# Routed rows of a mixture-of-experts layer in 25 blocks of 256 and 21 blocks of 128 rows instead of 39 blocks of 256

## The chip, the cores and the metric

One core of one Trainium2 chip. The metric is the device time of one launch in microseconds (us).

## The reference, cut to what matters

A decoder layer on 16 x 256 = 4096 tokens of width 256: linear attention, cross attention to 77 context rows, and a feed-forward part with one shared expert and 8 routed ones, of which each token takes the best two. Only the last part is touched.

```python
for e in range(N_EXPERTS):                          # 8, hidden width 1024
    h = new_gelu(xf @ Wfc[e] + bfc[e]) @ Wproj[e] + bproj[e]
    routed = routed + h * gate[:, e:e + 1]          # gate is 0 but for the token's two experts
return shared + routed
```

## The kernel before

Three stages follow each other.

1. **Attention**, 16 steps, until about 266 us.
2. **Shared expert**, `NSH` = 16 blocks of 256 tokens. Beside it VectorE works out the routing in small parts (`route(part)`, one behind each of the first four slices of blocks 0 to 3): how many rows each expert gets, which block belongs to which expert (`blk_expert`) and at which row of a DRAM table `rows_by_expert` each token's two copies go. Then GpSimd sends the 64 half-tiles of rows there with indirect DMAs, spread by `gelu_done` over the shared blocks 4 to 14.
3. **Routed experts**, `NRT` = 39 blocks of 256 rows. The rows of an expert fill whole blocks, the last one of each expert with padding, so 2 x 4096 / 256 + 7 = 39 blocks hold every split of the rows. All 39 are always computed.

A block G runs through `FC` = 8 slices f of 128 hidden units. Its way **up** (TensorE, `up`) is six matmuls of 256 columns into one PSUM bank (two halves of the contraction, by three products of the high and low f16 parts). ScalarE applies gelu into `g32` (L697), VectorE splits the result into a high and a low f16 part (L973, L974; together a pair of buffers `gs[f % 4]`, `g_ready`). The way **down** (TensorE, `down`) is six matmuls of 256 columns, three for each tile of 128 rows, and runs two slices behind: up of slice f, then down of slice f - 2. Two PSUM banks (`hid[f % 2]`) hold what comes up, two (`ysum`) what goes down.

Around a routed block n (block G = 16 + n) stand these, each in the order of its engine's own instruction stream:

- VectorE, behind slice 2: `evacuate(G - 1)`: y = ysum / scale + b2 for both tiles (L945), `y_read`, then times the gate (L954), `y_ready`. Behind slice 6: it reads the next block's expert number and copies gates and token numbers out of `meta` (L994, L996), `meta_taken`.
- SyncE: load `meta` of a block (L458, waits for `meta_taken` of the block before it), then load its rows transposed (`load_xT`, L464, into `xT[n % 2]`, waits until block n - 2 is up), then `load_b2` of an earlier block (L432, waits for `y_read`). Since they stand in one stream, the rows of block n + 3 aren't asked for until VectorE has taken the meta of block n + 2 in block n + 1.
- GpSimd: wait for `y_ready` and for all adds before it, one small operation (L560), then for each tile an indirect DMA that adds 128 rows to the output (L563).
- TensorE reads the expert number at the start of a block (L1186), waits for `xT_loaded` and works out weight addresses on the way.

## Time and profile before

| | before |
|---|---|
| median of 3 runs | 862.61 us (862.16 to 863.20) |
| profiled execution | 864.7 us, of it span 863.0 us |
| busy TensorE / VectorE / ScalarE / GpSimd | 797.6 / 632.9 / 356.8 / 240.6 us |
| granted TensorE clock, mean | 0.97 |
| stages | attention to 266 us, shared blocks to 441.55, routed blocks to 852.1, tail to 863.0 |

The span is the profiler's window on the execution, the profiled time is 1.7 us longer. A busy engine is one with an instruction open; matmuls overlap in the records, so how fast they follow each other is read from the distance of their starts, not from their durations.

### The profile page before, as it was taken

The numbers are of one execution on the slowest core, as the hardware profiler recorded it, in microseconds if no ns is written. First come the engines' busy times: TensorE is split into PE (matmuls) and PEld (weight loads), VectorE is DVE, ScalarE is ACT, GpSimd is POOL, SyncE is SP. The second block draws the span as 40 slices with busy tenths as digits, with TensorE's granted clock in tenths as the row PEclk, the third lists the DMA queues.
The fourth block names the chain that finished last, engine by engine and source line by source line (L and its number), as shares of the span: only waits on it lengthen the run. The fifth ranks groups of instructions, "written<-read, shape, count | busy, mean of one in ns | idle before, by whom it ended". The sixth has DMA issues, their size and how long they took to land.

```text
span 863.0 us, 21653 instructions
## 1 busy us (share of the span) xinstructions
PE 797.6 (92%) x6791; PEld 671.2 (78%) x6791; DVE 632.9 (73%) x2006; ACT 356.8 (41%) x777; POOL 240.6 (28%) x221
## 2 busy tenths in 40 slices
PE   3889898899856999999999999999999999999994
PEld 1666676666644888888888888888888888888884
DVE  4578888988756998888876666666666666666663
ACT  4445454454323555555543333333333333333331
POOL 2210101101110025555503333333333333333333
PEclk9999999999956999999999999999999999999998
DMA  5465676765333567887743434355344434444430
GB/s 178 141 159 137 180 150 170 168 155 119 81 62 84 156 180 239 235 237 238 234 120 62 65 55 69 58 57 70 54 64 63 66 64 63 63 62 64 65 50 7
DMA packets 168045, 98.07 MB, mean 114 GB/s; under 512 B 110316, under 2 KB 163336, under 8 KB 167944
## 3 DMA queue, kind: packets, MB, share of 16 engines
q1 hardware_dynamic: 153640, 79.65, 38.3%
q0 software_dynamic: 14304, 17.10, 11.5%
q8 instruction: 61, 1.00, 0.5%
q14 instruction: 40, 0.33, 0.1%
HBM read 37.84 MB, written 37.88 MB: 88 GB/s over the span
## 4 chain that ended last, share of the span: by engine, by line
PE 67%; issue 22%; DVE 5%; DMA 2%; SPq 1%; ACT 1%; POOL 1%; POOLq 0%; DVEq 0%; ACTq 0%
PE bank_kv L1177 11%; PE bank_st L1163 11%; PE bank_kv L1179 11%; PE bank_st L1165 11%; PE bank_kv L1178 11%; PE bank_st L1164 11%; DMA stage_w<-in_L_ffn_Wfc_s 1%; POOL rstd L519 1%; DVE w_parts L961 1%; DVE w_parts L740 1%; PE bank_st L1097 1%; DVE expert_buffers L973 1%; DMA expert_buffers<-rows_by_expert 0%; SPq L345 0%; PE bank L1116 0%
## 5 line engine op out<-in xcount | busy, mean ns | idle before, releaser
L697 ACT ACTIVATE expert_buffers<-bank_st,bias_columns 128x256 f32<-128x256 f32 x440 | 207.0, 473 | 334.2 <-DVE expert_buffers L974 214.5
L1177 PE MATMUL bank_kv<-w_parts,expert_buffers 128*128 (+1 forms) x880 | 240.6, 273 | 1.0 <-DVE expert_buffers L974 1.0
L1178 PE MATMUL bank_kv<-w_parts,expert_buffers 128*128 (+1 forms) x880 | 240.4, 273 | 0.0
L1179 PE MATMUL bank_kv<-w_parts,expert_buffers 128*128 (+1 forms) x880 | 240.4, 273 | 0.0
L973 DVE TENSOR_SCALAR expert_buffers<-expert_buffers 128x256 f16<-128x256 f32 x440 | 130.2, 296 | 120.4 <-ACT expert_buffers L697 100.2
L974 DVE SCALAR_TENSOR_TENSOR expert_buffers<-expert_buffers 128x256 f16<-128x256 f32 x440 | 188.6, 429 | 15.1
L1163 PE MATMUL bank_st<-expert_buffers,w_parts 128*128 128x256 f16 x624 | 170.1, 273 | 1.3 <-DMA expert_buffers<-rows_by_expert 1.3
L1165 PE MATMUL bank_st<-expert_buffers,w_parts 128*128 128x256 f16 x624 | 170.1, 273 | 0.0
L1164 PE MATMUL bank_st<-expert_buffers,w_parts 128*128 128x256 f16 x624 | 170.1, 273 | 0.0
L563 POOL DMA_INDIRECT out<-expert_buffers,token x78 | 121.8, 1561 | 20.6 <-issue 20.2
L1177 PEld LDWEIGHTS bank_kv<-w_parts,expert_buffers 128*128 128x128 f16 x880 | 86.2, 98 | 15.1 <-DVE expert_buffers L974 2.9
L1179 PEld LDWEIGHTS bank_kv<-w_parts,expert_buffers 128*128 128x128 f16 x880 | 86.3, 98 | 10.3
L1178 PEld LDWEIGHTS bank_kv<-w_parts,expert_buffers 128*128 128x128 f16 x880 | 86.3, 98 | 9.9
L544 POOL DMA_INDIRECT rows_by_expert<-rows,dest_rows x64 | 66.6, 1041 | 96.2 <-ACT expert_buffers L697 82.9
L560 POOL TENSOR_TENSOR wait_carrier<-minus_half 128x1 f32<-128x1 f32 x39 | 17.5, 448 | 267.5 <-DVE expert_buffers L954 267.5
L519 POOL TENSOR_TENSOR rstd<-var_eps,minus_half 128x6 f32<-128x6 f32 x21 | 27.8, 1326 | 216.0 <-DVE var_eps L835 216.0
L1163 PE MATMUL bank_st<-w_parts 128*128 128x256 f16 x256 | 71.1, 278 | 0.0
L1164 PE MATMUL bank_st<-w_parts 128*128 128x256 f16 x256 | 71.0, 277 | 0.0
L1165 PE MATMUL bank_st<-w_parts 128*128 128x256 f16 x256 | 71.0, 277 | 0.0
L1163 PEld LDWEIGHTS bank_st<-expert_buffers,w_parts 128*128 x624 | 61.0, 98 | 8.6 <-issue 1.6
L1165 PEld LDWEIGHTS bank_st<-expert_buffers,w_parts 128*128 x624 | 61.1, 98 | 7.1
L1164 PEld LDWEIGHTS bank_st<-expert_buffers,w_parts 128*128 x624 | 61.1, 98 | 7.0
(150 smaller groups left out, 1027.0 us busy)
## 6 DMA issues: line engine op xcount, KB each, us to landing
rows_by_expert<-w_parts SPq DMA_DIRECT2D x13, 795.0 KB, 5.5
stage_w<-in_L_ffn_Wfc SPq DMA_DIRECT2D x16, 512.0 KB
stage_w<-in_L_ffn_Wproj SPq DMA_DIRECT2D x16, 512.0 KB
expert_buffers<-in_L_ffn_bproj SPq DMA_DIRECT2D x39, 128.0 KB
rows<-in_x SPq DMA_DIRECT2D x16, 256.0 KB, 3.2
x_residual<-rows SPq DMA_DIRECT2D x16, 256.0 KB, 4.7
expert_buffers<-x_residual SPq DMA_DIRECT2D x16, 256.0 KB
out<-expert_buffers SPq DMA_DIRECT2D x16, 256.0 KB
```

What stands on the lines that cost most here:

```text
L519: pool.tensor_tensor(rstd[:, :], var_eps[:, :], minus_half[:, :], ALU.pow)\
L544: pool.indirect_dma_start(out=rows_dram, out_offset=bass.IndirectOffsetOnAxis(ap=dest[:, j, t:t + 1].bitcast(U32), axis=0), in_=rows[:, t, ...
L563: pool.indirect_dma_start(out=out_rows, out_offset=bass.IndirectOffsetOnAxis(ap=token[slot][:, t:t + 1].bitcast(U32), axis=0), in_=ybuf[sl ...
L697: act.activation(g32[f % 2], hid[f % 2][:, 0:BLK], ACT.Gelu_apprx_tanh, bias=bias, scale=UNSCALE).then_inc(s["gelu_done"], 1)
L973: chain(dve.tensor_scalar(g[:, 0, :], g32[f % 2], A_SCALE, None, ALU.mult), "g_hi", c + 1)
L974: dve.scalar_tensor_tensor(g[:, 1, :], g32[f % 2], A_SCALE, g[:, 0, :], ALU.mult, ALU.subtract)\
L1163: pe.matmul(out_f, w_hi, x_hi, start=k == 0, stop=False)
L1164: pe.matmul(out_f, w_hi, x_lo, start=False, stop=False)
L1165: op = pe.matmul(out_f, w_lo, x_hi, start=False, stop=k == DK - 1)
L1177: pe.matmul(y, g[:, 0, tile(t)], w_hi, start=f == 0 and t == 0, stop=False, skip_group_check=True)
L1178: pe.matmul(y, g[:, 0, tile(t)], w_lo, start=False, stop=False, skip_group_check=True)
L1179: op = pe.matmul(y, g[:, 1, tile(t)], w_hi, start=False, stop=f == FC - 1, skip_group_check=True)
```

## The change

The 39 routed blocks of 256 become `FULL` = 25 blocks of 256 rows and `HALF` = 21 blocks of 128, 71 row tiles instead of 78. Each expert gets its full blocks first, and what remains of its rows in half blocks. 16 + 25 + 21 blocks run in one stream.

- In a half block the six matmuls up have 128 columns. The way down multiplies the high part by both weight parts side by side, in one matmul of 512 columns, and the low part by the high weights in one of 256: two matmuls a slice. It runs six slices behind (`LAG_HALF`).
- VectorE splits the gelu outputs of two slices at once (still 256 columns), and evacuates behind slice 5 in three dependent operations, since the two products now lie in separate halves of the bank. It takes the next meta behind slice 7.
- Ways up use four PSUM banks instead of two in all blocks.
- The routing has 20 parts instead of 16, reaching into shared block 4.
- The sends to `rows_by_expert` go over shared blocks 5 to 14 (10 blocks instead of 11); the last is released by the same gelu.
- The loops of SyncE and GpSimd over routed blocks are unrolled. 12 padding stores instead of 13.

```diff
-    NRT = 2 * T // BLK + E - 1
+    FULL = (2 * T - E * (BLK - 1) + BLK - 1) // BLK
+    HALF = 2 * T // P + E - 1 - FULL * TB
+    NRT = FULL + HALF
-    SEND_FROM, SEND_BLOCKS = 4, 11
+    SEND_FROM, SEND_BLOCKS = 5, 10
+        FIRST_HALF = NSH + FULL
+        LAG_FULL, LAG_HALF = 2, 6
@@ ScalarE @@
+                    if G >= FIRST_HALF:
+                        pair = (c - FC * FIRST_HALF) // 2
+                        spare = g32[pair % 2]
+                        at = slice(f % 2 * P, f % 2 * P + P)
+                        if f % 2 == 0:
+                            act.wait_ge(s["g_ready"], FC * FIRST_HALF + pair - 1 if pair < 2 else c - 2)
@@ VectorE, evacuate @@
+                if G >= FIRST_HALF:
+                    y = ybuf[parity][:, 0, :]
+                    chain(dve.scalar_tensor_tensor(y, ysum[parity][:, 0, :], UNSCALE, b2blk, ALU.mult, ALU.add),
+                          "y_part", G - FIRST_HALF + 1)
+                    dve.scalar_tensor_tensor(y, ysum[parity][:, 1, :], UNSCALE, y, ALU.mult, ALU.add)\
+                        .then_inc(s["y_read"], 1)
+                    dve.wait_ge(s["y_read"], G + 1)
+                    dve.tensor_scalar(y, y, gate[parity][:, 0:1], None, ALU.mult).then_inc(s["y_ready"], 1)
+                    return
@@ VectorE, body @@
-                    if isinstance(G, int) and G < 4 and f < 4:
+                    if G < 5 and f < 4:
                         route(4 * G + f)
-                    if f == 2 and not (isinstance(G, int) and G == 0):
+                    if f == (2 if G < FIRST_HALF else 5) and G > 0:
-                    if f == 6 and next_kind(G, routed) == "routed":
+                    if f == (6 if G < FIRST_HALF else 7) and next_kind(G, routed) == "routed":
@@ TensorE @@
-                if not (isinstance(c, int) and c < 2):
-                    pe.wait_ge(s["gelu_done"], c - 1)
+                if c >= 4:
+                    pe.wait_ge(s["gelu_done"], c - 3)
+                if G >= FIRST_HALF:
+                    g = gs[(c - FC * FIRST_HALF) // 2 % 4][:, :, f % 2 * P:f % 2 * P + P]
+                    y = bank_kv[:, parity, :].rearrange("p (l n) -> p l n", l=2)
+                    both = w2[:, ds(e * 4096 + ((f // 4) * 2048), 2048)].rearrange("p (l n) -> p l n", l=2)
+                    both = both[:, :, (f % 4) * 256:(f % 4) * 256 + D]
+                    pe.matmul(y, g[:, 0, :], both, start=f == 0, stop=False, skip_group_check=True)
+                    pe.matmul(y[:, 0, :], g[:, 1, :], both[:, 0, :], start=False, stop=f == FC - 1, skip_group_check=True)\
+                        .then_inc(s["down_done"], 1)
+                    return
```

**Routing parts.** Before, `route` had 24 operations, now 41. Of the 17 added, 13 work on 8 columns (one count for each expert), three on 256 columns (whether a row lies beyond the full blocks, and the jump that it then makes), and the comparison that gives `blk_expert` is cut in two (200 and 168 columns where there was one of 312).

How the change stands in the instruction streams. TensorE, in a routed block before: the end of a way up, the way down of the slice two behind, the next way up (`bank_st` is `hid`, `bank_kv` is `ysum`).

```order
L1165 MATMUL bank_st<-expert_buffers,w_parts 128x256
L1177 REGISTER_ALU [waits g_ready]
L1177 MATMUL bank_kv<-w_parts,expert_buffers 128x256
L1178 REGISTER_ALU
L1178 MATMUL bank_kv<-w_parts,expert_buffers 128x256
L1179 MATMUL bank_kv<-w_parts,expert_buffers 128x256
L1177 MATMUL bank_kv<-w_parts,expert_buffers 128x256
L1178 MATMUL bank_kv<-w_parts,expert_buffers 128x256
L1179 MATMUL bank_kv<-w_parts,expert_buffers 128x256
L1163 ISA [waits gelu_done]
L1163 MATMUL bank_st<-expert_buffers,w_parts 128x256
```

The same place in a half block:

```order
L1249 MATMUL bank_st<-expert_buffers,w_parts 128x128
L1263 REGISTER_ALU [waits g_ready]
L1263 MATMUL bank_kv<-w_parts,expert_buffers 128x512
L1264 MATMUL bank_kv<-w_parts,expert_buffers 128x256
L1247 ISA [waits gelu_done]
L1247 MATMUL bank_st<-expert_buffers,w_parts 128x128
L1248 MATMUL bank_st<-expert_buffers,w_parts 128x128
L1249 ISA
L1249 MATMUL bank_st<-expert_buffers,w_parts 128x128
L1247 ISA
L1247 MATMUL bank_st<-expert_buffers,w_parts 128x128
```

Six matmuls down of 256 columns have become one of 512 and one of 256; those up still carry a weight load and every second one an address operation (ISA), and have half the columns.

VectorE in a routed block before, from the split of slice 3 to that of slice 6 and the taking of meta (L989 to L994); the evacuation stands right ahead of the first of these rows:

```order
L973 TENSOR_SCALAR expert_buffers<-expert_buffers 128x256 [waits down_done,gelu_done]
L974 SCALAR_TENSOR_TENSOR expert_buffers<-expert_buffers 128x256 [waits g_hi]
L973 TENSOR_SCALAR expert_buffers<-expert_buffers 128x256 [waits down_done,gelu_done]
L974 SCALAR_TENSOR_TENSOR expert_buffers<-expert_buffers 128x256 [waits g_hi]
L973 TENSOR_SCALAR expert_buffers<-expert_buffers 128x256 [waits down_done,gelu_done]
L974 SCALAR_TENSOR_TENSOR expert_buffers<-expert_buffers 128x256 [waits g_hi]
L973 TENSOR_SCALAR expert_buffers<-expert_buffers 128x256 [waits down_done,gelu_done]
L974 SCALAR_TENSOR_TENSOR expert_buffers<-expert_buffers 128x256 [waits g_hi]
L989 TENSOR_LOAD block_expert
L989 ISA x2
L994 ISA [waits y_added,meta_loaded]
L994 COPY gate<-expert_buffers 128x2
```

VectorE in a half block, from the split of slices 4 and 5:

```order
L1055 TENSOR_SCALAR expert_buffers<-expert_buffers 128x256 [waits down_done,gelu_done]
L1057 SCALAR_TENSOR_TENSOR expert_buffers<-expert_buffers 128x256 [waits g_hi]
L1010 SCALAR_TENSOR_TENSOR expert_buffers<-bank_kv,expert_buffers 128x256 [waits y_added,b2_loaded,down_done]
L1012 SCALAR_TENSOR_TENSOR expert_buffers<-bank_kv,expert_buffers 128x256 [waits y_part]
L1015 TENSOR_SCALAR expert_buffers<-expert_buffers,gate 128x256 [waits y_read]
L1055 TENSOR_SCALAR expert_buffers<-expert_buffers 128x256 [waits down_done,gelu_done]
L1057 SCALAR_TENSOR_TENSOR expert_buffers<-expert_buffers 128x256 [waits g_hi]
L1072 TENSOR_LOAD block_expert
L1072 ISA x2
L1078 ISA [waits y_added,meta_loaded]
L1078 COPY gate<-expert_buffers 128x1
L1080 COPY token<-expert_buffers 128x1
```

There were four splits between the last operation of the evacuation and the taking of meta; now there is one, and the three operations of the evacuation (L1010, L1012, L1015) each wait for the one before.

SyncE before, one turn of its loop: meta of a block, its rows transposed, and the expert number for the b2 of the block before:

```order
L457 REGISTER_ALU
L458 ISA [waits meta_taken]
L458 DMA expert_buffers<-rows_by_expert 128x2x9
L463 ISA
L464 ISA [waits up_done]
L464 DMA_TRANSPOSE expert_buffers<-rows_by_expert 128x4x256
L468 ISA
L468 TENSOR_LOAD block_expert
```

SyncE in the half blocks:

```order
L492 DMA expert_buffers<-rows_by_expert 128x9 [waits meta_taken]
L500 DMA_TRANSPOSE expert_buffers<-rows_by_expert 128x4x128 [waits up_done]
L504 TENSOR_LOAD block_expert
L504 ISA x2
L466 ISA [waits y_read]
L466 DMA expert_buffers<-in_L_ffn_bproj 128x256
```

The order of the three loads is the same, the address operations are gone, and the transposed tile has 128 rows instead of 256.

## Rows read from the trace of the kernel before

**Rows 1.** The page: busy time of each engine, share of the span, instructions.

```profile
PE 797.6 (92%) x6791; PEld 671.2 (78%) x6791; DVE 632.9 (73%) x2006; ACT 356.8 (41%) x777; POOL 240.6 (28%) x221
```

**Rows 2.** Busy by stretch (PE, PEld, DVE, ACT, POOL, clock, DMA, GB/s): routed, shared.

```profile
620.00:710.00 90.00, 90.00 (x827) 80.65 (x826) 60.68 (x190) 32.50 (x69) 28.62 (x25) 1.00 0.41 64
...
292.00:302.50 10.50, 10.13 (x93) 8.76 (x92) 10.09 (x27) 5.27 (x10) 0.00 (x0) 1.00 0.49 153
302.50:313.00 10.50, 10.04 (x93) 8.76 (x91) 10.06 (x28) 5.58 (x10) 0.00 (x0) 1.00 0.52 164
```

**Rows 3.** Timeline of TensorE (start, length in us): the same matmul of two successive blocks.

```profile
600.39 0.27 PE L1163 MATMUL bank_st<-expert_buffers,w_parts 128*128 128x256 f16 x1
...
610.87 0.27 PE L1163 MATMUL bank_st<-expert_buffers,w_parts 128*128 128x256 f16 x1
```

**Rows 4.** Timeline of TensorE in one attention step: matmuls of other widths.

```profile
155.45 0.45 PE L1140 MATMUL bank<-w_parts 128*128 128x8 f16 x12
...
159.53 0.39 PE L1059 MATMUL bank<-w_parts 128*128 128x77 f16 x6
159.76 2.75 PE L1069 MATMUL bank_kv<-w_parts 128*128 128x512 f16 x12
162.35 1.47 PE L1076 MATMUL bank<-w_parts 128*128 128x256 f16 x12
```

**Rows 5.** Source lines L1140 and L1059: durations ns min/median/max of one instruction.

```profile
L1140 PEld LDWEIGHTS bank<-w_parts x192: 95/96/147, 73.8 to 265.8; 128*128 128x128 f16 x192
L1140 PE MATMUL bank<-w_parts x192: 166/166/211, 74.0 to 265.8; 128*128 128x8 f16 x192
...
L1059 PE MATMUL bank<-w_parts x192: 196/199/267, 50.6 to 250.6; 128*128 128x77 f16 x192
```

**Rows 6.** Timeline of VectorE in a routed block.

```profile
603.50 0.75 DVE L945 SCALAR_TENSOR_TENSOR expert_buffers<-bank_kv,expert_buffers 128x256 f32<-128x256 f32 x2
604.29 0.62 DVE L954 TENSOR_SCALAR expert_buffers<-expert_buffers,gate 128x256 f32<-128x256 f32 x2
604.82 0.29 DVE L973 TENSOR_SCALAR expert_buffers<-expert_buffers 128x256 f16<-128x256 f32 x1
...
605.48 0.29 DVE L973 TENSOR_SCALAR expert_buffers<-expert_buffers 128x256 f16<-128x256 f32 x1
...
608.40 0.43 DVE L974 SCALAR_TENSOR_TENSOR expert_buffers<-expert_buffers 128x256 f16<-128x256 f32 x1
609.23 0.17 DVE L994 COPY gate<-expert_buffers 128x2 f32 x1 [0.40 <-DMA out<-expert_buffers,token]
609.30 0.16 DVE L996 COPY token<-expert_buffers 128x2 int32<-128x2 int32 x1
```

**Rows 7.** ScalarE's groups: busy us, mean ns of one | idle before.

```profile
L697 ACT ACTIVATE expert_buffers<-bank_st,bias_columns 128x256 f32<-128x256 f32 x440 | 207.0, 473 | 334.2 <-DVE expert_buffers L974 214.5 <-PE bank_st L1165 108.3 <-issue 11.3
L580 ACT ACTIVATE w_parts<-bank 128x154 f32<-128x154 f32 x16 | 4.7, 294 | 3.3 <-PE bank L1107 3.3
```

**Rows 8.** SyncE's queue, timeline of DMA issues.

```profile
440.47 0.37 SPq L458 DMA_DIRECT2D expert_buffers<-rows_by_expert  x1
440.89 1.24 SPq L464 DMA_TRANSPOSE expert_buffers<-rows_by_expert  x1
...
609.64 0.38 SPq L458 DMA_DIRECT2D expert_buffers<-rows_by_expert  x1
```

**Rows 9.** DMA issues of the span: median us from issue to landing.

```profile
expert_buffers<-rows_by_expert SPq DMA_TRANSPOSE x39, 3.2
...
w_parts<-rows SPq DMA_TRANSPOSE x32, 2.5
```

**Rows 10.** Timeline of GpSimd: the last block's adds.

```profile
854.00 1.56 POOL L563 DMA_INDIRECT out<-expert_buffers,token  x1
855.86 1.55 POOL L563 DMA_INDIRECT out<-expert_buffers,token  x1 [0.30 <-issue]
```

**Rows 11.** VectorE's groups: two routing operations, on 256 and on 8 columns.

```profile
L906 DVE TENSOR_TENSOR w_parts<-w_parts 128x256 f32<-128x256 f32 x1 | 0.4, 421 | 0.0
...
L900 DVE TENSOR_SCALAR w_parts<-w_parts 128x8 int32<-128x8 int32 x1 | 0.2, 172 | 0.0
```

More of the change, by code:

```diff
@@ L60, in decoder_layer, with tiles_in, rows_of, sent @@
     PADS = 3
[L61 to L63 removed]
+    SEND_FROM, SEND_BLOCKS = 5, 10
+    PAD_STEPS = (ROW_TILES + PADS * TB - 1) // (PADS * TB)
+    assert FULL == 25 and HALF == 21 and PAD_STEPS < B
     assert S == 256 and D == 256 and H == 1024 and CK <= P
[L66 to L67 removed]
+    rows_dram = nc.dram_tensor("rows_by_expert", [PAD_STEPS * PADS * TB * P, ROW], F32).ap()
+    rows16_dram = rows_dram.bitcast(F16)[:, 0:2 * D]
     x2_dram = nc.dram_tensor("x2_residual", [T, D], F32).ap()
+    def tiles_in(n):
+        return TB if n < FULL else 1
+    def rows_of(n):
+        first = n * BLK if n < FULL else FULL * BLK + (n - FULL) * P
+        return slice(first, first + tiles_in(n) * P)
+    def sent(n):
+        return sum(tiles_in(m) for m in range(n)) * 16
     def tiles_of(ap, b):
@@ L223, in decoder_layer @@
         base = scratch(TE).rearrange("p (e t) -> p e t", e=E)
+        beyond = gated
         place = te(scratch(TE))
@@ L1191, in body @@
                 e = expert_of(G - NSH) if routed else E
-                if before != "routed":
-                    e_before = E
-                else:
-                    e_before = expert_of(G - (NSH + 1)) if at_start else held[0]
-                held[0] = e
+                experts[G] = e
+                lag = LAG_FULL if G < FIRST_HALF else LAG_HALF
                 for f in range(FC):
@@ L1202, in body @@
                     up(G, parity, e, f)
-                    if f >= 2:
-                        down(G, parity, e, f - 2)
-                    elif before is not None:
-                        down(G - 1, 1 - parity, e_before, FC - 2 + f)
+                    d = FC * G + f - lag
+                    if d >= 0 and not (G == FIRST_HALF and f < LAG_HALF - LAG_FULL):
+                        down_lagging(d)
                     if f == 1 and isinstance(G, int) and G == 0:
@@ L1216, in body @@
                 if is_last(G):
-                    for f in range(FC - 2, FC):
-                        down(G, parity, e, f)
+                    for d in range(FC * NBLK - lag, FC * NBLK):
+                        down_lagging(d)
             pe.wait_ge(s["x1_ready"], B)
```

195 lines of the change are left out of this document (121 added, 74 removed).

## The prediction

> **What bounds the kernel now.** I read the busy times first, then the stretches, then the timelines of single engines. TensorE is busy for 797.6 of 863.0 us, VectorE for 632.9 [rows 1]. The stretches say where that matters: from 620 to 710 us TensorE is busy for 90.00 of 90.00 us at a granted clock of 1.00, VectorE for 60.68 and GpSimd for 28.62; in the shared blocks around 300 us VectorE is busy for 10.09 of 10.50 us and TensorE already stands still for 0.37 [rows 2]. So the routed stage is bound by TensorE alone, and the part of the shared stage that carries the routing is bound by VectorE. The timeline of TensorE gives the price of a routed block: the same matmul comes 10.48 us later in the next block [rows 3], which is 96 matmuls of 256 columns at 109.2 ns from start to start. All 39 blocks are the same.
>
> **What is removed.** 39 blocks become 25 of the same kind. 14 x 10.48 = 146.7 us go.
>
> **What a half block costs TensorE.** It has 48 matmuls up of 128 columns, 8 down of 512 and 8 of 256. No row shows one of 128 columns in f16, so I bound its distance from the rows at other widths. For 512 columns it is (162.35 - 159.76) / 12 = 215.8 ns [rows 4]; with 109.2 for 256 that is 106.6 ns for each 256 columns and 2.6 ns besides. So 128 columns take 53.3 + 2.6 = 55.9 ns, if nothing else shows up when matmuls get short. What could is the weight load, since each matmul has its own. The rows with short matmuls speak to that: twelve of 8 columns fill 0.45 us, the last being 0.166 long, so they start 0.284 / 11 = 26 ns apart, each with its load of a full 128 x 128, which is recorded as 96 ns long; six of 77 columns start (0.39 - 0.199) / 5 = 38 ns apart, 6 ns over their 32 ns of columns [rows 4, 5]. Loads of 96 ns thus overlap. With those 6 ns I get 59.3 as the other end for 128 columns. I take 55.9, since the matmuls here stand in long runs like the ones of 256. A half block is then 48 x 0.0559 + 8 x (0.2158 + 0.1092) = 2.68 + 2.60 = **5.28 us** (5.45 at the other end). The five address operations of a slice have half the time of before to run ahead in. They were hidden before, and I add nothing for them; the first rival prices them together with the weight loads.
>
> **What a half block needs around it.** The block has half the time, but the chain that brings in the next rows doesn't halve. Rows of block n + 3 are asked for by SyncE only behind the meta of block n + 3, and that waits until VectorE has taken the meta of block n + 2 behind slice 7 of block n + 1. I follow it from the start of slice 5 in block n + 1:
> - gelu of slice 5 done after about 1.0 us: matmuls up 0.34, the way through the array and a semaphore about 0.3, gelu 0.37 (473 ns at 256 columns, a copy of 154 columns takes 294 [rows 7]; an estimate between them)
> - VectorE: the split of slices 4 and 5, 0.66 until the next operation may start (604.82 to 605.48); the evacuation, whose operations overlapped in pairs (0.75 for two, 0.62 for two) and now each wait for the one before, about 1.2; the split of slices 6 and 7, 0.75; reading the expert number and the two copies, 0.40 + 0.23 [rows 6]
> - SyncE: 0.18 until the meta is issued (609.46 to 609.64), 0.42 until the transposing load (440.47 to 440.89) [rows 8]
> - the load: 3.2 us from issue to landing for 256 rows, 2.5 for the transposes of 128 rows in the attention stage [rows 9]; I take 2.5, since the size is the same, though those start in SBUF and these in DRAM
> - 0.1 until TensorE starts.
>
> That is 7.5 us, from a point 5 x 0.66 = 3.3 us into block n + 1, and the end is the start of block n + 3. Two blocks can't be shorter than 10.8 us, one not than **5.4**. That is 0.12 more than TensorE needs. So I expect TensorE to wait a little for its rows at each half block: 21 x 5.4 = 113.4 us. If the landing is under 2.2 the chain is covered and it is 21 x 5.28 = 110.9; with the landing of 3.2 and 0.2 more on SyncE it is 5.85 and 122.9. Behind the waiting TensorE nothing else is late, since every other chain hangs on it. VectorE itself has about 4 x 0.66 + 1.2 + 0.64 = 4.5 us of work for each half block, GpSimd one add, which starts 1.86 us after the one before where two follow each other [rows 10], and about 0.7 ahead of it: both below 5.4.
>
> **Routing.** VectorE gets 13 more operations on 8 columns at 0.172 + 0.04 of waiting, three on 256 columns at 0.42 + 0.04 [rows 11], and about 0.3 for the comparison cut in two: 2.75 + 1.4 + 0.3 = 4.4 us. They fall into shared blocks 1 to 4, where VectorE has 0.4 us to spare in 10.5 [rows 2]. Nothing hides them there but the slack of about 1 us that the way down has, two slices behind, and block 4, which had no routing before. Of the four blocks I count 8 x 0.66 = 5.3 us of splits, 1.5 of evacuation and 2.5 of weight conversion each, 37.2 together (10.09 of 10.50 with some routing among it [rows 2]); with the routing of before, 6.3 by its groups, and the added 4.4 it is 47.9 against 41.9 us of TensorE's work, 6.0 over, where three blocks were 2.8 over before. TensorE's added wait is **+3.2 us**, with 2 and 4.4 as bounds. Below nothing it can't go.
>
> **The end.** The last block has one add instead of two; the second started 1.86 us behind the first [rows 10], and both lie behind the last matmul. **-1.9 us.** The six slices of lag at the end are matmuls that are counted already. They wait for the split of slices 6 and 7 about as long as the old ones did: 0. The sends end behind the same gelu as before, and one padding store less lies beside the attention: 0. Four PSUM banks change nothing for full blocks, where TensorE didn't wait: 0.
>
> **Sum.** -146.7 + 113.4 + 3.2 - 1.9 = -32.0. The profiled execution (864.7, span 863.0) would become 832.7 and 831.0; on the median of 862.6, which lies 0.4 us below the span and 2.1 below its own time, it gives **830.6 us**.
>
> **Rivals.**
> - *The matmuls of 128 columns show part of their weight loads.* Halfway between 55.9 ns and the recorded length of a load, at 76 ns, a half block takes 48 x 0.076 + 2.60 = 6.25 us, 21 of them 131.2, and the kernel 862.6 - 146.7 + 131.2 + 3.2 - 1.9 = 848.4. For it: no row has this width, and TensorE's address operations stand between the loads. Against it: 26 and 38 ns at shorter widths. The Trainium skill, page "TensorE: Matmul & The Clock Gate", section "Back-to-back issue gap", gives about 81 ns for a sustained stream of load and matmul at 128 columns, against 56 for isolated ones; by it a half block would take 6.49 us and the kernel 853. By that rule much of the gain would go, though this trace's 38 ns at 77 columns speak against it.
> - *They show them in full, and the kernel gets slower.* At 96 ns, the recorded load, a half block takes 7.21 us, 21 take 151.4, more than the 14 full ones gave, and the kernel 868.6. It decides from (146.7 + 1.9 - 3.2) / 21 = 6.92 us for a half block, 90 ns a matmul. The same rows speak against it.
> - *The chain of loads is longer than I count it*, because the landing stays near 3.2 us or VectorE comes late: 5.85 us, 862.6 - 146.7 + 122.9 + 3.2 - 1.9 = 840.1. The load runs beside adds, meta and b2 loads that are as many for half the rows.
> - *Nothing waits*: 5.28 us and routing at its lower bound of 2: 826.9.
>
> **How the numbers follow.** The forecast's own case, 827.5 to 835, has 0.60; the longer chain, 835 to 842, 0.14; loads partly shown, 842 to 861, 0.12; slower 0.06; under 827.5, 0.08. The range of 826 to 848 leaves out the slower case, the upper half of the loads' case and the last bit below, some 0.16. Changes under 0.2% can't be told from none here. Faster by more: 0.93. Within: 0.01. Slower: 0.06.
>
> **What would show it.** Half blocks 5.3 to 5.5 us apart in TensorE's timeline, matmuls up 56 to 59 ns apart. Where TensorE idles, it is at the start of a half block, released by the DMA of `rows_by_expert`, about 0.1 us a time; waits in the middle of a block, for `g_ready` or gelu, would show the chain wrong. Full blocks still 10.48 us. Shared blocks 1 to 4 together 3 us longer, with VectorE busy throughout. One add behind the last matmul. The prediction fails if the distance of matmuls up is over 65 ns, or the landing of the half transposes over 3 us.

## The result, and the profile after

The changed kernel takes 849.89 us (median of 4 runs, 847.65 to 851.07) against 862.38 us before: ratio 0.985, 95% interval 0.9817 to 0.9883. That is faster, by 12.5 us where the prediction had 32, and outside its range of 826 to 848. The profiled execution took 847.65 us, of it span 845.9.

The page after, busy times (beside [rows 1]):

```profile
PE 769.6 (91%) x6791; PEld 628.9 (74%) x6791; DVE 627.3 (74%) x1988; ACT 365.7 (43%) x833; POOL 228.6 (27%) x221
```

The stretches after (columns as in [rows 2]): full routed blocks, two shared blocks, half blocks.

```profile
620.00:710.00 90.00, 90.00 (x844) 80.59 (x843) 61.78 (x190) 33.32 (x73) 29.09 (x25) 1.00 0.42 64
292.00:302.50 10.50, 9.77 (x89) 8.17 (x87) 9.98 (x29) 5.10 (x9) 0.00 (x0) 1.00 0.52 143
302.50:313.00 10.50, 9.16 (x81) 7.29 (x80) 9.95 (x28) 5.09 (x9) 0.00 (x0) 1.00 0.45 133
710.00:835.00 125.00, 114.96 (x1290) 86.30 (x1288) 84.17 (x265) 59.12 (x161) 39.37 (x42) 1.00 0.40 61
```

Full blocks are what they were. In the half blocks TensorE stands still for 10 of 125 us, at the full clock (granted 1.00, which is 2.4 GHz), and no other engine is full. Where it stands still, its timeline shows (the start of a half block, and the second slice behind it):

```profile
760.02 0.38 PE L1263 MATMUL bank_kv<-w_parts,expert_buffers 128*128 x1
760.24 0.27 PE L1264 MATMUL bank_kv<-w_parts,expert_buffers 128*128 x1
760.94 0.23 PE L1247 MATMUL bank_st<-expert_buffers,w_parts 128*128 128x128 f16 x1 [0.43 <-DMA expert_buffers<-rows_by_expert]
761.00 0.22 PE L1248 MATMUL bank_st<-expert_buffers,w_parts 128*128 128x128 f16 x1
761.06 0.23 PE L1249 MATMUL bank_st<-expert_buffers,w_parts 128*128 128x128 f16 x1
761.19 0.23 PE L1247 MATMUL bank_st<-expert_buffers,w_parts 128*128 128x128 f16 x1
...
761.75 0.22 PE L1247 MATMUL bank_st<-expert_buffers,w_parts 128*128 128x128 f16 x1
761.80 0.22 PE L1248 MATMUL bank_st<-expert_buffers,w_parts 128*128 128x128 f16 x1
761.86 0.22 PE L1249 MATMUL bank_st<-expert_buffers,w_parts 128*128 128x128 f16 x1
761.91 0.22 PE L1247 MATMUL bank_st<-expert_buffers,w_parts 128*128 128x128 f16 x1
761.97 0.22 PE L1248 MATMUL bank_st<-expert_buffers,w_parts 128*128 128x128 f16 x1
762.02 0.22 PE L1249 MATMUL bank_st<-expert_buffers,w_parts 128*128 128x128 f16 x1
762.08 0.38 PE L1263 MATMUL bank_kv<-w_parts,expert_buffers 128*128 x1
```

In a long run the matmuls of 128 columns start 0.055 us apart, the one of 512 holds the array for 0.22 and that of 256 for 0.11: the array time of the prediction. A slice is 0.66, eight are 5.28. But between two blocks there is a gap, 0.70 us from the last matmul down to the first up where 0.11 would do, and the first slice behind it is slower by 0.15 (0.81 from 760.94 to 761.75). From start to start half blocks take 6.10 us in the median, 6.19 in the mean (18 intervals; the first two, 5.34 and 6.32, in which the stage of full blocks ends, are left out here and below). The row names the rows' DMA as releaser of 0.43 us. The waits of TensorE and of its weight loads between 710 and 835 us put most down to something else (total us, times, longest):

```profile
PEld bank_st L1247 <- issue: 17.8, 21, 1.9
```
```profile
PE bank_st L1247 <- DMA expert_buffers<-rows_by_expert: 6.2, 9, 1.5
PE bank_st L1247 <- ACT expert_buffers L733: 3.6, 10, 0.4
```

"Issue" stands at the start of each of the 20 half blocks behind the first (at one of them twice), so the profile shows nothing that the weight load waited for: TensorE's own instruction stream was late. What stands there is the read of the expert number, L1284. Its line in the trace, in half blocks and around 760 us after, then in full blocks and around 608 us before (PEldq is the stream, durations in ns):

```profile
L1284 PEldq TENSOR_LOAD <-block_expert x19: 296/302/642, 715.5 to 827.4; - x19
L1284 PEldq FUSED_REGOPS  x19: 151/151/151, 716.2 to 827.7; - x19
L1284 PEldq SEQ_ASSERT  x19: 18/18/18, 716.5 to 827.9; - x19
...
L1284 PEldq TENSOR_LOAD <-block_expert x1: 302/302/302, 760.0 to 760.0; - x1
L1284 PEldq SEQ_ASSERT  x1: 18/18/18, 760.6 to 760.6; - x1
```
```profile
L1186 PEldq TENSOR_LOAD <-block_expert x1: 577/577/577, 607.8 to 607.8; - x1
L1186 PEldq SEQ_ASSERT  x1: 26/26/26, 608.6 to 608.6; - x1
```

Before, the read began at 607.8 and the block's first matmul at 609.23: the stream was 1.4 us ahead of the array, and the read, longer than after, was hidden. After, it begins at 760.0, as the last way down enters the array (760.02 and 760.24). It ends at 760.6, and the array restarts at 760.94. The stream has lost its lead. What fills it in the half blocks, besides matmuls and loads, are address operations (line L1249, 710 to 830 us):

```profile
L1249 PEldq FUSED_REGOPS  x310: 46/46/46, 710.4 to 829.9; - x155
```

L1247 has as many, so a slice has four of them, with one of 32 ns for the way down: 4 x 46 + 32 = 216 ns in a slice of 660. The starts of these operations show the lead in every slice. Before, an address operation of L1163 begins 0.5 us ahead of its matmul in slice 0, right behind the read, and 0.8 to 1.2 us ahead from slice 2 on (medians): the stream wins its lead back. In the half blocks it is 0.10 us in slice 0 and 0.2 to 0.4 in slices 1 to 7, and it hardly grows there.

**Where the time went**, by the two traces: from the start of the first half block (705.07) to the end of the last matmul (836.54) it is 131.5 us; the last full block before ran 1.9 us past its 10.48, so the half blocks cost 129.6 us, not 113.4. The shared stage is 2.3 us longer (175.74 to 178.00 from the first matmul up of shared block 0 to that of routed block 0; blocks 1 to 4 +3.6, block 0 -2.5, the others +1.1). The last matmul's end to the span's end fell from 10.9 to 9.4; the attention is 0.7 shorter. -146.7 + 129.6 + 2.3 - 1.5 - 0.7 = -17.0, and the spans differ by 17.1. The medians differ by 12.5 alone, because the profiled execution lies 2.3 us above its median before and 2.2 below it after.

### The profile page after: what moved, and what is told of

The parts are those of the page before. It is cut to its first block, busy times and chain, and to the rows that moved or that the text cites. A ratio compares the mean times of both kernels' runs of the same rounds, so it can differ in the third digit from the quotient of the medians.

```text
span 845.9 us, 21759 instructions
## 1 busy us (share of the span) xinstructions
PE 769.6 (91%) x6791; PEld 628.9 (74%) x6791; DVE 627.3 (74%) x1988; ACT 365.7 (43%) x833; POOL 228.6 (27%) x221
## 4 chain that ended last, share of the span: by engine, by line
PE 51%; issue 25%; DVE 10%; DMA 10%; ACT 2%; POOL 1%; SPq 1%; POOLq 0%; ACTq 0%; DVEq 0%
PE bank_kv L1270 7%; PE bank_kv L1271 7%; PE bank_kv L1272 7%; PE bank_st L1247 5%; DMA expert_buffers<-rows_by_expert 5%; PE bank_st L1249 4%; PE bank_st L1248 4%; PE bank L1247 4%; PE bank L1249 4%; PE bank L1248 4%; PE bank_kv L1263 3%; DMA stage_w<-in_L_ffn_Wproj 2%; DVE w_parts L1034 2%; DVE expert_buffers L1047 2%; PE bank_kv L1264 1%
## 5 line engine op out<-in xcount | busy, mean ns | idle before, releaser
L1270 PE MATMUL bank_kv<-w_parts,expert_buffers 128*128 (+1 forms) x656 | 179.0, 273 | 5.0 <-DVE expert_buffers L1048 4.7
L733 ACT ACTIVATE expert_buffers<-bank_st,bias_columns 128x256 f32<-128x256 f32 (+1 forms) x248 | 108.1, 437 | 166.3 <-PE bank_st L1249 119.2
L1272 PE MATMUL bank_kv<-w_parts,expert_buffers 128*128 (+1 forms) x656 | 178.8, 273 | 0.0
L1271 PE MATMUL bank_kv<-w_parts,expert_buffers 128*128 (+1 forms) x656 | 178.8, 273 | 0.0
L733 ACT ACTIVATE expert_buffers<-bank,bias_columns 128x256 f32<-128x256 f32 (+1 forms) x248 | 108.2, 436 | 142.2 <-PE bank L1249 76.6
L1047 DVE TENSOR_SCALAR expert_buffers<-expert_buffers 128x256 f16<-128x256 f32 x328 | 101.7, 310 | 78.1 <-ACT expert_buffers L733 76.9
L1048 DVE SCALAR_TENSOR_TENSOR expert_buffers<-expert_buffers 128x256 f16<-128x256 f32 x328 | 139.4, 425 | 11.3
L1247 PE MATMUL bank_st<-expert_buffers,w_parts 128*128 128x256 f16 (+1 forms) x368 | 88.3, 249 | 11.3 <-DMA expert_buffers<-rows_by_expert 7.5
L1249 PE MATMUL bank_st<-expert_buffers,w_parts 128*128 128x256 f16 (+1 forms) x368 | 88.4, 249 | 0.0
L1248 PE MATMUL bank_st<-expert_buffers,w_parts 128*128 128x256 f16 (+1 forms) x368 | 88.0, 248 | 0.0
L1249 PE MATMUL bank<-expert_buffers,w_parts 128*128 128x256 f16 (+1 forms) x368 | 87.1, 248 | 0.0
L1248 PE MATMUL bank<-expert_buffers,w_parts 128*128 128x256 f16 (+1 forms) x368 | 87.0, 248 | 0.0
L1247 PE MATMUL bank<-expert_buffers,w_parts 128*128 128x256 f16 (+1 forms) x368 | 87.0, 248 | 0.0
L1270 PEld LDWEIGHTS bank_kv<-w_parts,expert_buffers 128*128 128x128 f16 x656 | 64.1, 98 | 17.4 <-DVE expert_buffers L1048 9.6
L1272 PEld LDWEIGHTS bank_kv<-w_parts,expert_buffers 128*128 128x128 f16 x656 | 64.2, 98 | 7.5
L1271 PEld LDWEIGHTS bank_kv<-w_parts,expert_buffers 128*128 128x128 f16 x656 | 64.2, 98 | 7.1
L1263 PE MATMUL bank_kv<-w_parts,expert_buffers 128*128 x168 | 63.3, 378 | 0.5 <-DVE expert_buffers L1057 0.5
L1153 PE MATMUL bank_kv<-w_parts 128*128 128x512 f16 x192 | 47.6, 401 | 13.2 <-DMA w_parts<-w_parts 13.2
```

The costliest lines, as they stand in the source:

```text
L733: act.activation(spare[:, at], hid[c % 4][:, 0:width(G)], ACT.Gelu_apprx_tanh, bias=bias, scale=UNSCALE).then_inc(s["gelu_done"], 1)
L1047: chain(dve.tensor_scalar(g[:, 0, :], g32[f % 2], A_SCALE, None, ALU.mult), "g_hi", c + 1)
L1048: dve.scalar_tensor_tensor(g[:, 1, :], g32[f % 2], A_SCALE, g[:, 0, :], ALU.mult, ALU.subtract)\
L1247: pe.matmul(out_f, w_hi, x_hi, start=k == 0, stop=False)
L1248: pe.matmul(out_f, w_hi, x_lo, start=False, stop=False)
L1249: op = pe.matmul(out_f, w_lo, x_hi, start=False, stop=k == DK - 1)
```

## The experiments

Theories for the half block's 6.1 us. **A**: TensorE's own stream, that is the read of the expert number behind address operations that leave it no lead. **B**: the chain that brings the rows (meta, then transposed rows), longer than the prediction's 7.5 us; in this trace the transposing loads land after 2.9/3.4/4.8 us (min/median/max) where it took 2.5. The expectations have letters of their own. In runs 1, 2 and 5 theory A is the chain (B here) and B the loads themselves; S in runs 5 to 9 is A here; the stream was first put down as a theory for run 5, after runs 1 and 2 had come out against the chain.

Half blocks are given as mean and median from start to start. A static expert, or one read used for all half blocks, makes the half blocks multiply by another expert's weights. Only times of neighbouring runs compare well: the attention ends at 263 to 268 us in these traces, and in runs 5 to 9 the shared blocks 4 to 15 exceed their 10.48 us by 8.5 to 9.9 us in sum, in runs 1 to 4 and 10 by 2.9 to 5.4 (run 12 comes back to that). So the times of runs 5 to 9 are some 5 us longer for reasons outside the half blocks; what a run does to the half blocks is read from its trace.

**1. The rows asked for first.** SyncE's order in routed blocks:

```diff
                 load_xT(n + 2)
+                load_rows(n + 2)
                 load_b2(n + (1 + NSH), expert_of(n + 1))
-                if n + 3 < NRT:
-                    load_rows(n + 3)
```
(with the `load_rows(2)` ahead of the loop gone). The meta of block n + 2 then stands behind its rows.

> SyncE asks for the transposed rows of a block before the meta of that block, so that the load no longer waits for VectorE. Theory A (TensorE's waits in the half blocks come from the chain VectorE evacuates, splits, takes meta, then SyncE loads meta, then rows, which is 8.6 us long from slice 5 and closes over two blocks): the load is then issued when the block two ahead is up, has 5.3 us for 3.4 to 3.8 us, and half blocks come every 5.3 to 5.35 us instead of 6.2: 20 x 0.9 = 18 us less than the changed kernel, about 831. Theory B (the loads themselves, or the DMA engines, can't follow at this rate): half blocks stay above 5.9 us and the time above 844.

844.73 us, ratio 0.9793 (0.9753 to 0.9834), and not the 831 of the chain's theory. Half blocks 6.06/6.06: the outliers of up to 7.2 us are gone, the median hardly moved. The waits between 710 and 830 us:

```profile
PEld bank_st L1245 <- issue: 14.8, 20, 1.1
```

No wait for the rows' DMA is left, and the block's start is as late as ever. B explains the outliers, not the 6.06.

**2. Four slices behind instead of six**, the evacuation behind slice 3, which shortens the chain.

```diff
-        LAG_FULL, LAG_HALF = 2, 6
+        LAG_FULL, LAG_HALF = 2, 4
-                    if f == (2 if G < FIRST_HALF else 5) and G > 0:
+                    if f == (2 if G < FIRST_HALF else 3) and G > 0:
```

> The way down of the half blocks runs four slices behind instead of six, and VectorE evacuates behind slice 3 instead of 5, so that the evacuation no longer stands between the last gelu of a block and the taking of meta. Theory A: the split of slices 6 and 7 starts when its gelu is done, about 0.56 us earlier, the chain over two blocks is shorter by that, a half block by 0.28 (6.2 to 5.9): about 6 us less, 844, if the shorter lag brings no wait for the way down. Theory B (loads or DMA engines are the limit): no change, 850.

844.33 us, 0.9776 (0.9738 to 0.9814), half blocks 6.08/6.07. As in 1. The time is the one that the chain's theory named, but by luck: its half blocks were to take 5.9.

**3. Half blocks without their adds.** Leaves out the indirect DMAs that add the half blocks' rows to the output.

```diff
-                for t in range(tiles_in(n)):
+                for t in range(tiles_in(n) if n < FULL else 0):
```

> Leaves out the adds of the half blocks into the output (GpSimd's indirect DMAs of 21 blocks), so the output lacks those rows; all else stays. If the transposing loads land after 3.4 us instead of 2.5 because the add of the evacuated block runs beside them, they land after about 2.5, half blocks take 5.6 to 5.75 and the kernel about 839 with the missing last add. If the landing is the load's own, it stays at 3.3 to 3.4, half blocks at 6.0 to 6.1, and the time at 845 to 848.

842.48 us, 0.9776 (0.9736 to 0.9817). The transposes land faster, and half blocks stay at 6.11/6.06:

```profile
DMA to landing us min/median/max: 2.7/2.7/4.5
```

So the adds do lengthen the landing, from 2.7 us to the 3.4 of the changed kernel. That isn't what holds the array.

**4. One routing operation four times** (on 256 columns, in block 3), to see whether routing work is paid in full.

```diff
+                    for _ in range(4):
                         then(dve.tensor_tensor(beyond, place, over_t(full_rows), ALU.is_ge))
```

> One wide routing operation of VectorE in shared block 3 is done four times instead of once: 3 x 0.46 = 1.4 us more. If VectorE bounds the shared blocks with routing, blocks 1 to 4 take 1.4 us longer in TensorE's timeline and the kernel 851.3. If the added routing has slack to lie in, under 0.4 us.

850.01 us, 0.9876 (0.9818 to 0.9933). Block 3 took 13.81 us instead of 12.43: +1.38 for three operations of about 0.46. The whole shared stage took 178.59 us where runs 1 and 2, on the same chip, have 177.16 and 177.14: VectorE's added work there is paid one to one. The kernel's median moved by 0.1 us alone; 1.4 us lie within the scatter of its four runs (849.15 to 857.06).

**5. A static expert for TensorE in half blocks**, the order of SyncE as in the changed kernel. This removes the read and all the address operations.

```diff
-                e = expert_of(G - NSH) if routed else E
+                if G >= FIRST_HALF:
+                    e = G % E
+                else:
+                    e = expert_of(G - NSH) if routed else E
```

> On TensorE alone the half blocks use a fixed expert number (G modulo 8) instead of the one read from memory, so TensorE neither reads the number nor works out addresses in them; the output of those blocks is that of another expert. Theory A (the chain of VectorE and the loads of rows sets the half block, 8.6 us over 5.3 of lead): half blocks stay at 6.0 to 6.2 us, 850. Theory S (TensorE's own instruction stream sets it: reading the expert number takes 0.6 us at the start of each block, and the stream, with an address operation for every second or third matmul, doesn't get far enough ahead of the array to hide it): the 0.7 us at the block's start go, until the chain of the rows, 0.2 to 0.4 us behind it, is the limit: 5.6 to 5.85 us, about 842.

847.41 us, 0.9771 (0.9704 to 0.9839); half blocks 6.02/5.76. The waits of the weight loads from 710 to 835 us:

```profile
PEld bank_st L1247 <- DMA expert_buffers<-rows_by_expert: 15.4, 14, 2.7
...
PEld bank_st L1247 <- issue: 0.2, 1, 0.2
```

The wait on "issue" is gone and the rows' chain has taken its place, at 5.8 us in the median, with outliers up to 7.8: a second limit right behind the first. Behind such gaps, of up to 2.3 us, the first six matmuls up take 0.34 us, where they take 0.49 to 0.64 in the changed kernel. So the address operations themselves make the block's first slice longer, by 0.15 us or more.

**6. Both: static expert and rows first.**

> The same fixed expert number on TensorE in the half blocks, and SyncE asks for the rows before the meta. Theory S: both limits are gone, half blocks at 5.28 to 5.35 us, 21 x 0.75 under the rows-first kernel's 844.7: about 830. Theory D (the DMA landings, at 3.4 us, or VectorE, are the limit left): 5.6 or more, over 835.

831.89 us, 0.9605 (0.9565 to 0.9645); half blocks 5.33/5.28. With both limits out of the way most half blocks take exactly their array time. That the kernel also comes near the predicted 830.6 us is partly luck: its half blocks are 0.1 us under the predicted 5.4, and its shared blocks 4 to 15 exceed 10.48 us by 9.1 us where the changed kernel's trace has 4.5.

**7. The read ahead of slice 3 of the block before**, rows first: is it enough to read earlier?

```diff
+                    if f == 3 and FIRST_HALF <= G < NBLK - 1:
+                        experts[G + 1] = expert_of(G + 1 - NSH)
                     up(G, parity, e, f)
```
(and the block's start uses what was read.)

> Rows first, and TensorE reads the next half block's expert number ahead of slice 3 of the block before, addresses as before. If only the place of the read mattered (at the start of a block, where it meets the wait for the rows), the 0.6 us would be hidden and half blocks take 5.3 to 5.5: about 833. If the stream of instructions is the limit as a whole, the same 0.7 us come back in the middle of the block: 6.0 us, 844.

849.58 us, 0.9814 (0.9776 to 0.9852), half blocks 6.09/6.03. The slices' medians were 0.825, five or six of 0.66, 0.695, 1.195 in run 1; here 0.715, 0.66, 1.095, 0.81, 0.66, 0.66, 0.71, 0.66. The stall moved with the read, to the start of slice 3, and the waits of the weight loads from 710 to 830 us still say "issue":

```profile
PEld bank L1245 <- issue: 12.7, 20, 0.7
```

An earlier place doesn't help where the stream has so little lead anywhere: address operations begin 0.2 to 0.4 us ahead of their matmuls in most slices here too. Nor is it that the block's addresses wait for the number: the next block needs it only some 4 us later. The slices clear of the read still take 0.66 to 0.72 us, address operations and all.

**8. One read for all half blocks**, rows first. It was meant to take the read away and keep the address operations.

```diff
-                e = expert_of(G - NSH) if routed else E
+                if G > FIRST_HALF:
+                    e = experts[FIRST_HALF]
+                else:
+                    e = expert_of(G - NSH) if routed else E
```

> Rows first, and TensorE reads an expert number once, for the first half block, and uses it for all 21; the address operations stay. The output is that of another expert. Theory S: without the read the stream needs less than the array's 5.28 us: 5.3 to 5.45, about 831 to 834. If the address operations are the larger part, 5.6 to 5.9 and about 840.

840.60 us, 0.9716 (0.9667 to 0.9765); half blocks 5.64/5.29. But the trace shows that the address operations went with the read. A line of the ways up between 710 and 830 us (the changed kernel has 310 such operations on it, above):

```profile
L1247 PEldq FUSED_REGOPS  x8: 46/46/46, 710.1 to 712.6; - x8
```

All eight lie ahead of the second half block; with one number for all half blocks the addresses are worked out once. For TensorE this run is run 6 over again, and it doesn't separate the two. Twelve of 18 half blocks take 5.28 to 5.30; the others wait for the rows:

```profile
PEld bank_st L1245 <- DMA expert_buffers<-rows_by_expert: 7.9, 7, 1.5
```

Seven of its transposing loads landed after 4.4 to 5.1 us. Why these are so slow here and not in run 6 is not shown.

**9. The read kept, its result unused, no address operations**, rows first.

```diff
                 e = expert_of(G - NSH) if routed else E
+                if G >= FIRST_HALF:
+                    e = G % E
```

> Rows first; TensorE reads the expert number at the start of each half block but doesn't use it: addresses are those of a fixed expert, without address operations (the output of those blocks is another expert's). Theory S says that the read (about 0.65 us) and the address operations (8 x 4 x 46 + 8 x 32 ns = 1.7 us) are both in the way only together: without the operations the stream runs far enough ahead to hide the read, and half blocks take 5.28 to 5.4 us, 832. If the read stops the array by itself (because it waits until the queue is empty, say), 0.6 us stay: 5.9 us, 844.

839.68 us, 0.9712 (0.969 to 0.9735), half blocks 5.35/5.28. The line of the read in half blocks, and around 760 us:

```profile
L1282 PEldq TENSOR_LOAD <-block_expert x21: 296/306/594, 713.3 to 819.4; - x21
...
L1282 PEldq TENSOR_LOAD <-block_expert x2: 297/300/302, 760.0 to 765.6; - x2
```

It reads as long as in the changed kernel, but begins 1.6 us ahead of its block (761.64), and 1.2 us or more in all; with the address operations it is 0.85 to 0.9 in most blocks, and the gap itself is part of that: there the read begins only 0.2 us ahead of the last matmul down, here 1.1 to 1.5. **So the read costs nothing where no address operations stand beside it** (9). Read and address operations together cost 6.05 - 5.28 = 0.77 us a half block, 16 us in 21 (run 1 against 6 and 9). Theory A holds, and B is the limit right behind it. No run has the address operations without the read. That they alone would be hidden over a whole block is likely, since in run 1 the six slices between the one behind the gap and the one ahead of the next take 0.66 to 0.70 us, but it is not shown.

The time of 839.68 us is 7.8 over run 6's with the same half blocks. In the traces 3.8 us of it are a longer attention, 0.8 the shared blocks, and 1.7 the first routed block, which waits for its rows.

**10. Rows first and four slices behind.**

> The changed kernel with the rows of block n + 2 asked for ahead of its meta of n + 3 (as in the run with rows first) and the half blocks' way down four slices behind with the evacuation behind slice 3 (as in the run with four slices). Theory A (the read of the expert number in TensorE's stream is exposed and sets 6.05 us per half block once the rows' chain is out of the way): no further gain, 843 to 845 us, half blocks 6.05 us. Theory B (the chain of rows still gave part of the 6.05): 838 to 841 us, half blocks below 5.9 us.

845.56 us, 0.9811 (0.9759 to 0.9863), half blocks 6.06/6.06: nothing beyond 1 or 2, as A has it. Runs 1, 2 and 10 are the best kernels here that leave nothing out, 18 to 19 us under the kernel before.

**11. Routing thinner, sends denser**: three parts of the routing in each of blocks 1 to 6, the sends over 8 blocks (7 to 14), rows first.

```diff
-    SEND_FROM, SEND_BLOCKS = 5, 10
+    SEND_FROM, SEND_BLOCKS = 7, 8
-                    if G < 5 and f < 4:
+                    elif 1 <= G < 7 and f in (0, 1, 3) and 3 * G + (0, 1, 3).index(f) + 1 < 20:
```

> Rows first, and the routing behind block 0 goes with three parts a block over shared blocks 1 to 6 instead of four a block over 1 to 4, with the sends over blocks 7 to 14. VectorE then has 6 blocks for the same work: by the theory that it bounds those blocks, TensorE's added wait of 4.9 us in blocks 1 to 4 falls to about 3, so the kernel is 1.5 to 2.5 us under the rows-first one (844.7, so 842 to 843), unless the denser sends cost it elsewhere.

859.96 us, 0.9963 (0.9943 to 0.9983), 17 us over what was expected. Blocks 1 to 6 exceed 10.48 us by 3.1 us in sum where run 1 had 5.0, so thinner routing gains 1.9. Blocks 7 to 14, with the denser sends, exceed it by 16.8. That raised a question on the change itself, whose four banks and ten blocks of sends the prediction counted at nothing.

**12. Those two edits alone in the kernel before.**

```diff
-    SEND_FROM, SEND_BLOCKS = 4, 11
+    SEND_FROM, SEND_BLOCKS = 5, 10
-        hid = [bank_st[:, c, :] for c in range(2)]
+        hid = [bank_st[:, 0, :], bank_st[:, 1, :], bank3[:, :], bank7[:, :]]
-                    pe.wait_ge(s["gelu_done"], c - 1)
+                    pe.wait_ge(s["gelu_done"], c - 3)
```
(and `hid[f % 4]` where it was `hid[f % 2]`). In the expectations from here on S means that the sends are the cause, K the banks, J only both together, and C the chip.

> The kernel before with two parts of the change alone: four PSUM banks for the way up, and the sends over blocks 5 to 14 instead of 4 to 14. Prediction of record: nothing, 862.6 +- 1. If the denser sends cost what the changed kernel shows in shared blocks 6 to 12 (1.1 us more than before), 863.7.

869.09 us, 1.007 (1.0049 to 1.0092): slower by 6 us. Then each alone, on another chip:

> The kernel before with its sends to rows_by_expert over shared blocks 5 to 14 (10 blocks) instead of 4 to 14, and nothing else; two PSUM banks for the ways up as before. Together with four banks this cost about 6 us (869.1 against 863.2). Theory S (the denser sends alone lengthen the shared blocks): about 868 to 869 us, the shared blocks with sends exceed 10.48 us by some 7 us in sum. Theory K (the four banks are what does it): 863 us, excess about 1.3 us as in the kernel before. Theory J (only both together): 863 here and in the run with four banks alone.

> The kernel before with four PSUM banks for the ways up in all blocks, sends over blocks 4 to 14 as before, and nothing else. Theory S: 862.5 to 863, no change. Theory K: 868 to 869 us, the shared blocks with sends exceed 10.48 us by some 7 us in sum. Theory J: 863.

863.95 us, 0.9999 (0.9975 to 1.0024), for the sends, 864.85 us, 1.0023 (0.9998 to 1.0049), for the banks. But the changed kernel in run 10, on the same chip, lost no more in its shared blocks than these two, so the chip could have been the reason. Hence the kernel before itself, with a trace, beside both edits, on one chip:

> The kernel before itself, unchanged, so that its trace and that of the next run come from one chip. Its shared blocks 4 to 15 exceeded 10.48 us by 2.8 us in sum in the trace that the prediction read. Theory C (how much the shared blocks lose is a property of the chip: the traces of the two other chips with 8 to 10 us lost it in every kernel): this sum lies within 1.5 us of that of the next run. Theory J (four banks and sends over ten blocks together lose it): about 3 to 5 us here.

> The kernel before with four PSUM banks for the ways up and the sends over blocks 5 to 14, as in the run that was 6 us slower on another chip. Theory J: again 1.005 to 1.009 of the kernel before, the shared blocks 4 to 15 exceed 10.48 us by some 8 us. Theory C: within 0.3% of the kernel before, with its sum of excess.

865.11 us, 1.0014 (0.9987 to 1.0041), and 871.31 us, 1.0075 (1.0051 to 1.0098); excess of blocks 4 to 15 over 10.48 us: 4.6 and 10.6. The waits for VectorE's splits at the way down, from 300 to 445 us, of the one and of the other:

```profile
PEld bank_kv L1177 <- DVE expert_buffers L974: 2.5, 8, 0.7
```
```profile
PEld bank_kv L1177 <- DVE expert_buffers L974: 12.1, 23, 1.4
```

Both edits together cost 6 us on such a chip, as J has it, and C is right in part: chips differ. The gaps between GpSimd's sends tell them apart (its line, idle without a releaser, us and times: the kernel before itself and both edits, then the sends alone):

```profile
  issue: 12.2, 34
```
```profile
  issue: 14.9, 43
```
```profile
  issue: 5.8, 19
```

Across the traces the gaps are 4 to 8.5 us on some chips (changed kernel, runs 1 to 4, 10, each edit alone) and 11 to 16 on the others (kernel before, runs 5 to 9, 11 and 12's both edits). The runs went over six chips, with two to four traces on each, all of one kind. On which chip the traces of the kernel before and of the changed kernel in the sections above were taken isn't known. Kernels with both edits (without run 11) exceed 10.48 us in blocks 4 to 15 by 2.9 to 5.4 us on the first and by 8.2 to 10.6 on the second. Each edit alone once more, on a chip of the first kind again:

> The kernel before with the sends over blocks 5 to 14 and nothing else, again, since on the chip of its first run nothing lost time in the shared blocks. Chips fall into two kinds by the gaps between GpSimd's sends: in some traces 5 to 8 us of gaps with no releaser before the 64 sends, in others 11 to 16. If this chip is of the second kind: theory J (only both edits together) 1.000 of before and an excess of the shared blocks 4 to 15 over 10.48 us of 3 to 5.5 us; theory S (the sends) 1.005 to 1.009 and 8 to 10.6 us. If it is of the first kind, as in its first run: 1.000 and about 5 us by either.

> The kernel before with four PSUM banks and nothing else, again. On a chip of the second kind: theory J 1.000 of before and an excess of 3 to 5.5 us; theory K (the banks) 1.005 to 1.009 and 8 to 10.6 us. On one of the first kind: 1.000 to 1.002 and about 5 us by either.

864.49 us, 1.0007 (0.9978 to 1.0037), and 862.26 us, 0.9989 (0.996 to 1.0018), with 2.9 and 1.8 us of excess. Whether one edit alone costs something on a chip of the second kind stays open, as does what the chips differ in.

## Why the prediction was right in sign and wrong in size

- **"14 x 10.48 = 146.7 us go"**: right, full blocks are 10.48 us still.
- **The array time of a half block, 5.28 us**: right, 48 matmuls up at 55 ns and 0.66 a slice; run 6 shows it undisturbed. The rival of weight loads that show comes near the measured time (848.4) by luck, for a reason that isn't there: in long runs matmuls of 128 columns stand 55 ns apart. The Trainium skill, page "TensorE: Matmul & The Clock Gate", section "Back-to-back issue gap", has about 81 ns a matmul for a sustained stream of weight loads and matmuls at 128 columns; the trace doesn't agree, with 55 ns.
- **"The five address operations of a slice have half the time of before to run ahead in. They were hidden before, and I add nothing for them"**: this is the step that failed. The words name the danger and then price it at nothing. The read of the expert number at the block's start, which the description of the kernel names, has no term at all. Together they cost 0.77 us a half block, 16 us (run 1 against runs 6 and 9), because with 128 columns the stream's lead stays at 0.2 to 0.4 us where it was 0.8 to 1.2, and the read with what belongs to it takes 0.47 and more. With the address operations gone the read is hidden (run 9); whether they would be hidden without the read is open.
- **The chain of rows, 5.4 us a half block**: mis-sized. It is 5.8 in the median (run 5), because the landing is 3.3 us there and 3.4 in the changed kernel, and not 2.5 (0.7 of the 3.4 from the adds, run 3), which is the rival with 5.85. It cost only the outliers here, about 21 x 0.13 = 3 us, since TensorE's stream is later still. The other links came as predicted: evacuation 1.18 us (760.12 to 761.30) for 1.2, reading and copies 0.40 + 0.22, SyncE 0.37 between the two loads.
- **Routing, +3.2 us**: +3.6 in blocks 1 to 4, and added work there is paid one to one (run 4). The match is in part luck: block 0 has 2.5 us less wait than in the trace that the prediction read. In sum over blocks 0 to 4 the excess rose from 5.2 to 6.4 us; in six of the eight traces of the kernel before, with run 12's edits or none, it is 3.5. So routing added between 1.2 and 2.9 us.
- **The end, -1.9**: -1.5.
- **"Four PSUM banks change nothing for full blocks, where TensorE didn't wait: 0"**, and the sends: 0. For the changed kernel's own trace this nearly holds, its shared blocks 5 to 15 exceed 10.48 us by 3.9 us where they had 2.8. On some chips both together cost 6 us in the shared blocks (run 12), where TensorE is not the only full engine. The prediction had looked at the routed blocks for the banks and at the last send for the sends.
- **What would show it**: "waits 0.1 us at the start of a half block, released by the DMA" was the wrong releaser and size; the text also said that it fails with a landing over 3 us, which came.

## What to carry to other kernels

In these traces TensorE's instruction stream runs ahead of the array by a lead (up to 1.4 us before, 0.2 to 0.4 in the half blocks), and register work is hidden only as far as that lead goes. When a change halves the matmuls' length but not their number, or the register work beside them, work out the stream's time too: from the line of each register read (PEldq here) take how far ahead of its block it begins, and ask what is left of it when the array needs half the time. Look at the trace of each experiment for whether its edit did what it was meant to: run 8's took away more. And where two limits lie within 0.3 us of each other a run that removes one shows only the other; take both away in one kernel, then put each back.

## What the runs showed of the hardware that was not expected

- A register read on TensorE's stream took 0.30 us and the operations behind it 0.15 and 0.02; from its start to the array's restart it was 0.85 to 0.9 us in most blocks (changed kernel). 32 address operations of 46 ns and 8 of 32 ns a half block of 128-column matmuls kept its lead at 0.2 to 0.4 us; beside matmuls of 256 columns it recovered to 0.8 to 1.2 us within two slices.
- Behind the gap the first six matmuls of 128 columns take 0.48 us (760.94 to 761.42), later six 0.33. It isn't the array that restarts slowly: with no address operations they take 0.34 behind gaps of up to 2.3 us (run 5).
- Transposing loads of 128 rows from DRAM land after 2.7 us with no adds beside them and 3.0 to 3.5 with them (medians), as long as 256 rows did (3.2 [rows 9]); their issue takes 1.22 us for 128 rows and 1.26 for 256 in the median.
- Chips differ in how densely GpSimd's indirect stores follow each other (gaps of 4 to 8.5 or 11 to 16 us over 64), and the two edits of run 12 cost the kernel before 0.7% on two chips of the second kind, while kernels that hold both exceed 10.48 us in the shared blocks 4 to 15 by 2.9 to 5.4 us on the first kind and by 8.2 to 10.6 on the second. The kernel before itself took 862.4 to 865.1 us on all (medians). What makes the difference is open.
